# A ring of 12 slots in place of 8 for gathered rows, in memory from the descriptor region

## The chip, the cores and the metric

One Trainium2 chip, one of its cores. The metric is the device time in microseconds (us) of one execution. The engines are called PE (TensorE, matrix products), DVE (VectorE), ACT (ScalarE), POOL (GpSimd) and SP (SyncE, which only issues DMAs).

## The reference

A graph layer with 6250 nodes and 100,000 edges, in float32, on rows of 128 features. The edges are sorted by their target `dst`; `src` is random.

```
hs, hd = x[src], x[dst]
a_k    = exp(relu([hs, hd] @ W_att_k + b_att_k))                 k = 1, 2, 3
avg    = (a_1 / att_1[dst] + a_2 / att_2[dst] + a_3 / att_3[dst]) / 3,   att_k = segment_sum(a_k, dst)
m      = avg * relu(relu(relu(hs @ W1 + b1) @ W2 + b2) @ W3 + b3)
h      = segment_sum(m, dst) / max(degree, 1)
out    = layernorm(x + relu([x, h] @ Wc1 + bc1) @ Wc2 + bc2)
```

The three message layers depend on the source node alone, and so does one half of each attention logit.

## The kernel before

**First stage (to about 55 us).** The messages and the source half of the logits are computed once per node and stored in HBM as a table, one row of 131 floats a node (128 message values and 3 logits, `ROW`). Beside it, POOL gathers plain rows of `x` for nine "early" half units (36 gathers, L558), whose messages are later computed from `x` without the table.

**Edge stage (55 to 776 us).** The 391 groups of 256 edges (`GROUP`, two tiles of 128) are worked off in 126 units (`first_order`, L131). The first unit is one pair of groups, the next 23 are long units of four groups (8 tiles), the other 102 are short ones of two groups (4 tiles; the last one has a single group). Every tile needs one indirect DMA of POOL (L1224) that fetches the 128 table rows which its edges name, 524 bytes each. Nine of the long units (3, 5, ..., 19) gather only their first half, since the other half is an early one: 558 gathers in all.

The gathered rows go to a ring in SBUF, `gath` (L606), of `RING` = 8 slots with 4 tiles each. A long unit takes two places of the ring, any other unit one (`places`, L1066). For every unit POOL waits until PE has finished the units whose slots it needs (L1218, on `s_sum`, which PE raises with the last L1409 matmul of a unit), and then issues the unit's gathers; `taken` (L1069) says which unit that is. Each slot has a semaphore of its own (`s_gath`, L725).

For unit i the other engines work in order:
- SP loads the edges' distances (`near`) and the target half of the logits (`q_eye`).
- PE spreads the target half over the edges (L1357).
- DVE reduces it (L1809), then waits for the gathered rows and adds their three logits (L1815). This is the first read of the ring.
- ACT takes the exponential (L1537) and copies the mask (L1577); DVE makes the weights (L1835, L1840).
- PE multiplies gathered rows and weights into sums (L1405, and L1409 for the attention sums); DVE adds these to `acc` (L1857).

Each engine's order is written out by hand in one loop over the steps i: at step i DVE does L1815 and the weights of unit i + 1, then the sums of unit i - 1, and PE the sums of unit i. A stall of DVE at L1815 holds all of DVE's later work.

Other work is laid between these steps. Steps 0 to 24 count the edges from the first 94 groups ("hot" groups, whose targets are the first 384 nodes) in a table of counts (PE L1426, DVE L1693 and L1706, ACT L1551). Steps 26 to 77 then pass over all 49 blocks of the message table and multiply them by counts times exponentials (PE L1443, ACT L1507 and L1516, DVE L1736); step 78 adds the result to `acc` (DVE L1753). After it the final blocks start: when all edges of 512 nodes are summed, PE (L867, L881, L888, L892, L898), ACT (L917) and DVE (L954, L972, L979, L989, L993) make the output of these nodes in eight steps laid over the next units, and SP loads their `x` ahead and stores the output. The last blocks end at 791.6 us, after the last unit.

A second pass over the edges stands in the code for inputs whose targets don't fit the windows; it does not run here.

All buffers of the edge stage stand one behind the other in one SBUF tile, `work`, of `WORK` = 7536 float32 words a partition; the ring is the first. The program is built with the default region for the descriptors of POOL's DMAs, 16 KB a partition of SBUF.

```
def taken(i, ring):
    return sum(at < place[i] + places[i] - ring for at in place) - 1

def rows_of(i):
    at = place[i] % RING * CHUNK
    return gath[:, at:at + n_tiles(i), :]

for n, u in enumerate(order):
    if taken(n, RING) >= 0:
        pool.wait_ge(s_sum, groups_to(taken(n, RING)))
```

Of the kernel before, what the change touches and what calls it, by code (L numbers as in the profile page):

```python
# [52 lines left out]
HOT_GROUPS = 94  # L53
HOT_WIDTHS = (6, 9, 10)
PAIRS = 4
RING = 8
TWO, THREE = 2, 3
AHEAD = 3
NEAR = 6
# [33 lines left out]
def gnn_program(nc, x, x_t, src, dst, w_first, w_rest, b_rows, table, hot_table, near_table, q_table, early_table, out,  # L93
# [59 lines left out]
    with ctx:  # L153
        def sb(name, shape, dt=f32):
            return ctx.enter_context(nc.sbuf_tensor(name, shape, dt))

        def sem(name):
            return ctx.enter_context(nc.semaphore(name))
# [101 lines left out]
        more = sb("more", [1, 1], i32)  # L260

        WORK = 7536
        work = sb("work", [P, WORK])

        def area(at, *dims):
            n = 1
            for d in dims:
                n *= d
            view = work[:, at:at + n]  # L270
            if len(dims) == 2:
                view = view.rearrange("p (a b) -> p a b", a=dims[0])
            if len(dims) == 3:
                view = view.rearrange("p (a b c) -> p a b c", a=dims[0], b=dims[1])
            if len(dims) == 4:
                view = view.rearrange("p (a b c d) -> p a b c d", a=dims[0], b=dims[1], c=dims[2])
            return view, at + n
# [9 lines left out]
        part_rest, at = area(at, n_blocks, HEADS)  # L287
        assert at <= WORK - COLS

        hot_logit_flat = hot_logit[:, :, :].rearrange("p j d -> p (j d)")
        staged = [logits_or_x[:, 0:COLS], work[:, WORK - COLS:WORK], hot_logit_flat[:, 0:COLS]]
        early_h, early_x, EARLY_BANK = staged[2], staged[1], 3
# [311 lines left out]

        gath, at = area(0, RING * CHUNK, ROW)  # L606

# [16 lines left out]
        hot_block, at = area(at, BLOCKS, 1 + ROW)  # L624
        assert at <= WORK

# [97 lines left out]
        s_least = sem("s_least")  # L724
        s_gath = [sem(f"s_gath{j}") for j in range(RING)]  # L725
        s_fill = sem("s_fill")
# [335 lines left out]
        def edge_pass(first):  # L1062
# [18 lines left out]
            def n_tiles(i):  # L1081
                return len(order[i]) * TILES
# [28 lines left out]
            def early_rows(k):  # L1111

                at = (place[early_units[k]] + 1) % RING * CHUNK
                return gath[:, at:at + CHUNK, 0:P]
# [18 lines left out]
# [5 lines that stand above are left out]
            def tiles_at(i, h):  # L1138

                return 0 if h and early(i) is not None else max(0, min(CHUNK, n_tiles(i) - h * CHUNK))  # L1140

            def rows_landed(eng, i):
                for h in range(places[i]):
                    if not tiles_at(i, h):
                        continue
                    slot = (place[i] + h) % RING
                    eng.wait_ge(s_gath[slot], 16 * sum(tiles_at(n, k) for n in range(i + 1) for k in range(places[n])
                                                       if (place[n] + k) % RING == slot))

# [863 lines left out]
```

## Time and profile before

| | |
|---|---|
| median of 3 runs | 998.15 us |
| lowest, highest run | 995.25, 999.38 us |
| span of the profiled execution | 791.6 us |
| median of the runs less the span | 206.6 us |
| own time of the profiled execution | not given beside its span |
| mean granted clock of TensorE | 0.885 |

Busy tenths of each engine in 40 slices of the span (19.8 us each), with the granted clock of TensorE, the DMA engines' share and what they moved:

```
PE   9952999999986779988889888887978887788885
DVE  5884678778887786777776777776677878787766
ACT  6656687777553426767677667661223233232323
POOL 7777777766577777777777777777777777777760
PEclk9985698988896775999999999999789989889898
DMA  7873333325742233333333333335234334333421
```

The span runs from the program's first to its last instruction on the engines; the rest of a run's time lies around it. A digit is the busy share of a slice in tenths, and 9 is 90% or more; PEclk is the clock that PE was granted, in tenths of full speed. Times in rows count from the span's start. "Idle before, and who ended it" counts only the time in which that engine itself stood still. An indirect DMA's row shows POOL's work on issuing it, not the transfer.

### The profile page before, as it was taken

Reading aid. Unit: us, or ns where it says so; the run is one execution under the profiler, and the core shown is the slowest. Engines: PE = TensorE matmul, PEld = TensorE weight load, DVE = VectorE, ACT = ScalarE, POOL = GpSimd, SP = SyncE. Lnnn points to the kernel's source line nnn. Section 1 sums busy time; section 2 is a strip of 40 time slices with the busy share of each in tenths; the row PEclk is TensorE's granted clock in tenths of the full one; section 3 lists DMA queues with packets and bytes.
Section 4 is the critical chain, followed back from the end, with each engine's and each line's share of the span. In section 5 each row is a group of like instructions: output and inputs, shape, how many; then the busy total and the mean of one; then the engine's idle time right before and its main releaser. Section 6 shows DMA issues by size and latency. Waiting matters only on the chain.

```text
span 791.6 us, 17405 instructions
## 1 busy us (share of the span) xinstructions
PE 663.7 (84%) x5133; PEld 520.8 (66%) x5133; DVE 582.3 (74%) x1943; ACT 420.1 (53%) x1048; POOL 571.1 (72%) x605
## 2 busy tenths in 40 slices
PE   9952999999986779988889888887978887788885
PEld 5741666666654556877778777775766765666664
DVE  5884678778887786777776777776677878787766
ACT  6656687777553426767677667661223233232323
POOL 7777777766577777777777777777777777777760
PEclk9985698988896775999999999999789989889898
DMA  7873333325742233333333333335234334333421
GB/s 241 237 200 78 81 84 80 79 68 62 70 81 58 70 96 75 87 79 78 79 84 80 82 80 78 77 76 135 66 96 111 105 105 134 105 104 104 98 59 34
DMA packets 82741, 75.14 MB, mean 95 GB/s; under 512 B 34872, under 2 KB 66400, under 8 KB 82640
## 3 DMA queue, kind: packets, MB, share of 16 engines
q0 software_dynamic: 19008, 39.82, 22.9%
q1 hardware_dynamic: 63344, 34.00, 15.6%
q8 instruction: 44, 0.72, 0.4%
q14 instruction: 57, 0.47, 0.2%
q10 hardware_dynamic: 288, 0.13, 0.1%
HBM read 64.62 MB, written 9.26 MB: 93 GB/s over the span
## 4 chain that ended last, share of the span: by engine, by line
DVE 30%; PE 27%; issue 14%; ACT 12%; POOL 7%; DMA 5%; DVEq 2%; SPq 1%; ACTq 0%
DVE fin L1736 9%; PE bank L1405 8%; ACT bank L1516 5%; POOL work L1224 5%; DVE acc L1857 3%; PE bank L1426 3%; DVE counts L1706 3%; PE bank L1409 3%; PE bank L881 2%; DVE fin L1693 2%; DVE work L1835 2%; DMA work<-message_table,src_t 2%; DVE fin L972 2%; DVE work L1840 2%; ACT work L1577 2%
## 5 line engine op out<-in xcount | busy, mean ns | idle before, releaser
L1224 POOL DMA_INDIRECT work<-message_table,src_t x558 | 530.2, 950 | 184.3 <-issue 164.8
L1405 PE MATMUL bank<-work 128*128 128x144 f32 (+8 forms) x1188 | 229.4, 322 | 41.7 <-DVE acc L1857 41.3
L1405 PEld LDWEIGHTS bank<-work 128*128 128x128 f32 x1188 | 181.9, 216 | 69.6 <-issue 55.9
L1577 ACT COPY work<-bank 128x192 f32<-128x192 f32 (+7 forms) x126 | 37.3, 296 | 207.1 <-DVE work L1809 206.0
L1443 PE MATMUL bank<-work,fin 128*128 128x129 f32 (+1 forms) x882 | 113.3, 284 | 0.0
L1857 DVE TENSOR_TENSOR acc<-acc,bank 128x192 f32 (+8 forms) x297 | 88.8, 299 | 30.4 <-issue 6.7
L1516 ACT ACTIVATE bank<-hot_logit 128x384 f32<-128x384 f32 (+1 forms) x147 | 72.7, 494 | 69.1 <-DVE fin L1736 61.3
L1443 PEld LDWEIGHTS bank<-work,fin 128*128 128x128 f32 (+1 forms) x882 | 104.2, 195 | 2.4 <-issue 0.6
L1840 DVE TENSOR_TENSOR work<-bank,work 128x576 f32<-128x576 f32 (+7 forms) x126 | 86.2, 684 | 13.5 <-DVE work L1835 0.5
L1736 DVE SCALAR_TENSOR_TENSOR fin<-bank,counts 128x384 f32<-128x384 f32 (+1 forms) x147 | 81.4, 554 | 18.1 <-ACT bank L1516 17.2
L1409 PE MATMUL bank<-work 128*4 128x48 f32 (+8 forms) x1188 | 92.3, 202 | 0.0
L1507 ACT ACTIVATE hot_logit<-logits_or_x,work 128x384 f32<-128x384 f32 (+1 forms) x147 | 88.3, 601 | 0.0
L881 PE MATMUL bank<-rest_w,acc 128*128 128x128 f32 x294 | 50.2, 334 | 29.4 <-DVE fin L972 26.4
L1409 PEld LDWEIGHTS bank<-work 128*4 128x4 f32 x1188 | 48.8, 87 | 35.8 <-issue 7.4
L881 PEld LDWEIGHTS bank<-rest_w,acc 128*128 128x128 f32 x294 | 44.6, 237 | 31.4 <-DVE fin L972 27.5
L1706 DVE TENSOR_TENSOR counts<-counts,bank 128x294 f32 (+2 forms) x94 | 56.2, 598 | 8.3 <-issue 7.3
L1357 PE MATMUL bank<-side 48*128 48x57 bf16 (+8 forms) x594 | 41.3, 185 | 22.6 <-DMA side<-logit_parts 18.0
L1551 ACT ACTIVATE fin<-fin 128x128 bf16<-128x128 f16 x188 | 59.4, 386 | 0.0
L1426 PE MATMUL bank<-fin 128*128 128x294 bf16 (+2 forms) x188 | 48.7, 396 | 11.5 <-ACT fin L1556 8.0
L1835 DVE TENSOR_SCALAR work<-work 128x12 f32<-128x12 f32 (+1 forms) x126 | 24.6, 195 | 42.4 <-ACT work L1537 40.4
L1693 DVE TENSOR_SCALAR fin<-fin 128x294 bf16<-128x294 f16 (+2 forms) x188 | 55.5, 338 | 0.0
L1767 DVE TENSOR_SCALAR side<-side,less_col 48x512 bf16<-48x512 bf16 x149 | 52.3, 364 | 3.3 <-DMA side<-near_nodes 3.2
(150 smaller groups left out, 769.0 us busy)
## 6 DMA issues: line engine op xcount, KB each, us to landing
work<-message_table,src_t POOLq DMA_INDIRECT x558
side<-near_nodes SPq DMA_DIRECT2D x102, 48.0 KB
side<-logit_parts SPq DMA_DIRECT2D x297, 0.8 KB
message_table<-work SPq DMA_DIRECT2D x12, 262.0 KB, 3.6
work<-message_table SPq DMA_DIRECT2D x48, 65.5 KB
work<-in_x_t SPq DMA_DIRECT2D x12, 256.0 KB, 4.2
fin<-in_x SPq DMA_DIRECT2D x11, 256.0 KB, 2.8
logits_or_x<-in_x_t SPq DMA_DIRECT2D x11, 256.0 KB, 3.5
```

Source lines behind the costliest of these rows:

```text
L881: last = pe.matmul(to[:, k * P:(k + 1) * P], acc[:, k, nodes], wc1[:, 1, :], start=True, stop=True)
L1224: pool.indirect_dma_start(out=rows_of(n)[:, t, :], out_offset=None, in_=table[:, :], in_offset=bass.IndirectOffsetOnAxis(ap=src_t[:, h, g: ...
L1405: pe.matmul(sums[:, at:at + HEADS * w], rows_here[:, t, 0:P], wt_of(i)[:, t, :], start=h == 0, stop=h == TILES - 1)
L1409: last = pe.matmul(sums[SUMS_AT:SUMS_AT + HEADS + 1, at + HEADS * w:at + HEADS * w + w], a_col[:, i % THREE, t, :], mask_of(i)[:, t, :], s ...
L1426: pe.matmul(bank[COUNT_BANKS[g % FOUR]][:, 0:n], hot_lo[:, t % HOT_RING, :], hot_comb[:, t % HOT_RING, 0:n], start=h == 0, stop=h == TILES ...
L1443: last = pe.matmul(bank[SIDE_BANKS[h]][:, k * (P + 1):(k + 1) * (P + 1)], hot_wt[0:m, b % THREE, k, h * P:(h + 1) * P], rows_here, start=F ...
L1507: act.activation(hot_logit[0:m, n % TWO, :], hot_ld[0:m, k, :], ACT.Relu, bias=hot_block[0:m, b % BLOCKS, 1 + P + k:2 + P + k]).then_inc(s ...
L1516: act.activation(bank[EXP_BANK][0:m, 0:hot_nodes], hot_logit[0:m, n % TWO, :], ACT.Exp).then_inc(s_he, 1)
L1706: dve.tensor_tensor(here, here, bank[COUNT_BANKS[g % FOUR]][:, 0:w * n_blocks].rearrange("p (b d) -> p b d", d=w), ALU.add).then_inc(s_cad ...
L1736: dve.scalar_tensor_tensor(hot_wt[0:m, b % THREE, k, :], bank[EXP_BANK][0:m, 0:hot_nodes], FLT_MAX, counts[0:m, b, :], ALU.min, ALU.mult). ...
L1840: dve.tensor_tensor(wt_of(i).rearrange("p t (k w) -> p t k w", w=w), from_q(i)[:, :, PARTS:PARTS + w].unsqueeze(2).to_broadcast([P, n, HEA ...
L1857: dve.tensor_tensor(here, here, sums[:, at:at + (HEADS + 1) * w].rearrange("p (k w) -> p k w", w=w), ALU.add).then_inc(s_acc, 1)
```

## The change

The ring gets 12 slots, and with it 12 semaphores in place of 8. The slots are 4 x 131 words each; four more are 2096 words, by which `work` grows to 9632 words (8384 bytes more a partition). The region for the descriptors of POOL's DMAs shrinks from 16384 to 4096 bytes a partition, which frees 12288. Every buffer behind the ring in `work` stands 2096 words further on. Where `RING` is used, the numbers follow: POOL's wait for a slot (`taken`), the slot and the semaphore of a unit, the wait of DVE before it writes early rows to a slot (L1821), and POOL's closing loop (L1228), which waits for the last 12 units' gathers in place of the last 8.

```diff
-RING = 8
+RING = 12
...
-        WORK = 7536
+        WORK = 9632
         work = sb("work", [P, WORK])
...
-    nc = bacc.Bacc("TRN2", target_bir_lowering=False, num_devices=1)
+    nc = bacc.Bacc("TRN2", target_bir_lowering=False, num_devices=1, dynamic_dma_scratch_size=4096)
```

## Rows read from the trace of the kernel before

**Rows 1.** The page: span, and busy us (share) and instructions of each engine
```profile
span 791.6 us, 17405 instructions
PE 663.7 (84%) x5133; PEld 520.8 (66%) x5133; DVE 582.3 (74%) x1943; ACT 420.1 (53%) x1048; POOL 571.1 (72%) x605
```

**Rows 2.** Waits, whole span: who waited for whom, us in total, times, longest
```profile
POOL work L1224 <- PE bank L1409: 19.5, 17, 5.7
DVE work L1815 <- DMA work<-message_table,src_t: 18.7, 12, 4.0
```

**Rows 3.** The gather line: count, ns min/median/max, first and last start
```profile
L1224 POOL DMA_INDIRECT work<-message_table,src_t x558: 938/944/2104, 55.2 to 768.6; - x186
```

**Rows 4.** Waits of POOL in 150 to 263 us
```profile
POOL work L1224 <- PE bank L1409: 16.4, 7, 5.7
```

**Rows 5.** Timeline of POOL: start, us, instruction, idle before and releaser
```profile
164.69 0.94 POOL L1224 DMA_INDIRECT work<-message_table,src_t  x1 [3.69 <-PE bank L1409]
...
270.60 0.97 POOL L1224 DMA_INDIRECT work<-message_table,src_t  x1 [0.30 <-issue]
...
535.50 0.94 POOL L1224 DMA_INDIRECT work<-message_table,src_t  x1 [0.30 <-issue]
```

**Rows 6.** Line L1815 in 290:536, 535:590, 590:745 and 745:792 us, with its waits
```profile
L1815 DVE TENSOR_TENSOR work<-work x53: 170/172/174, 290.3 to 535.7; 128x12 f32<-128x12 f32 x53
...
  DMA work<-message_table,src_t: 7.7, 5
...
  DMA work<-message_table,src_t: 0.6, 1
...
L1815 DVE TENSOR_TENSOR work<-work x6: 167/172/179, 748.5 to 773.9; 128x12 f32<-128x12 f32 x5, 128x6 f32<-128x6 f32 x1
...
  DMA work<-message_table,src_t: 5.3, 4
```

**Rows 7.** Timeline of DVE: first reads of gathered rows
```profile
290.28 0.17 DVE L1815 TENSOR_TENSOR work<-work 128x12 f32<-128x12 f32 x1
...
538.43 0.17 DVE L1815 TENSOR_TENSOR work<-work 128x12 f32<-128x12 f32 x1
...
546.54 0.17 DVE L1815 TENSOR_TENSOR work<-work 128x12 f32<-128x12 f32 x1 [4.03 <-DMA work<-message_table,src_t]
...
578.02 0.17 DVE L1815 TENSOR_TENSOR work<-work 128x12 f32<-128x12 f32 x1 [1.36 <-DMA work<-message_table,src_t]
...
763.61 0.18 DVE L1815 TENSOR_TENSOR work<-work 128x12 f32<-128x12 f32 x1 [2.29 <-DMA work<-message_table,src_t]
```

**Rows 8.** Waits of PE in 554:572, 572:592, 743:764 and 764:792 us
```profile
PE bank L1405 <- DVE acc L1857: 3.4, 1, 3.4
...
PE bank L881 <- DVE fin L972: 4.0, 1, 4.0
...
PE bank L867 <- DVE acc L1857: 2.3, 1, 2.3
PE bank L881 <- DVE fin L972: 0.4, 1, 0.4
...
PE bank L881 <- DVE node_sums L954: 2.8, 1, 2.8
```

**Rows 9.** By stage: us, busy us of each engine, PEclk, DMA share, GB/s
```profile
313.00:536.00 223.00, 197.32 (x1806) 172.44 (x1806) 159.03 (x465) 155.89 (x371) 168.62 (x179) 0.99 0.33 80
536.00:592.00 56.00, 46.65 (x371) 37.54 (x369) 37.47 (x127) 10.62 (x38) 42.28 (x46) 0.82 0.37 98
592.00:743.00 151.00, 124.89 (x994) 101.78 (x992) 119.04 (x432) 46.64 (x152) 114.21 (x121) 0.91 0.42 110
```

**Rows 10.** Timeline of POOL: two of its three longest gathers
```profile
78.89 2.10 POOL L1224 DMA_INDIRECT work<-message_table,src_t  x1 [0.30 <-issue]
...
760.58 1.46 POOL L1224 DMA_INDIRECT work<-message_table,src_t  x1 [0.30 <-issue]
```

**Rows 11.** The early gathers (L558): the longest ones, and issue to landing
```profile
L558 POOL DMA_INDIRECT hot_logit<-in_x,src_t x12: 940/944/1774, 14.9 to 51.3; - x12
...
DMA to landing us min/median/max: 3.2/4.0/4.8
```

## Prediction

> **What bounds the kernel now.** I read the page's busy shares first, then the waits, then the gather line, then the timelines of GpSimd (POOL) and of VectorE (DVE), then TensorE's (PE) waits by stage. In the shares [rows 1] no engine is full: PE is busy for 84% of the span, POOL for 72%. But POOL's share hides a saturated queue. Its 558 gathers take 944 ns each in the median [rows 3] and are 0.30 us apart (the idle in brackets of an undisturbed gather [rows 5] is that), so one leaves each 1.25 us: 558 x 1.25 = 697 us of the 714 us from the first to the last start [rows 3]. The other 17 us are almost all one thing: 19.5 us waited for PE's L1409, the matmul whose end frees a ring slot [rows 2]. In the stretch 150 to 263 us there are seven such waits, 16.4 us [rows 4], the first before the gather at 164.69 [rows 5]; seven usual spaces of 0.30 us are in them, so the ring itself costs 16.4 - 2.1 = **14.3 us** of POOL's time. From 262 us on POOL never stops.
>
> Who suffers? In L1815 DVE adds the gathered logits, so it is the first reader of a unit's rows. It reads unit 25 at 290.28 [rows 7], whose last gather began at 270.60 and ended at 271.57 [rows 5]: 18.7 us ahead. It reads unit 78 at 538.43, whose last gather ended at 536.44: 2.0 us. So between them the consumers (DVE and PE) outrun POOL: 53 units from 290.3 to 535.7 with no wait for rows [rows 6], 245.4 / 52 = 4.72 us each, against 4 x 1.25 = 5.0 us. The lead that POOL had is eaten at about 0.3 us a unit. From then on rows come late: 7.7 us of waits in 535 to 590, 0.6 in 590 to 745, 5.3 in 745 to 792 [rows 6], 13.6 in all of the 18.7 us [rows 2]; the other 5.2 us are the first two units, which the ring can't help. The kernel is consumer-bound until 536 us and short of rows in two places after it.
>
> **The change, part by part.** *Four more slots.* A long unit uses two places, a short one uses one. POOL may now be 12 places ahead of the units that PE has finished, not 8. While the nine early units alternate with the others, four places are one full long unit (8 gathers) and one early one (4): 12 gathers, 12 x 1.25 = 15.0 us; later they are 16 gathers, 20 us. The stalls to cover sum to 14.3 us, so all seven go, just. Two more slots, 7.5 us, would not do. POOL's 406 gathers from 261.9 us then run 14.3 us earlier, as long as PE's times up to 262 us stay as they are; nothing there waits for rows, so I let them stay.
>
> *What the earlier rows are worth.* Not 14.3 us: only where somebody waits for rows and PE, the busiest engine, is idle for it. Wait by wait, the smaller of DVE's wait and PE's idle time behind it:
> - 546.54, 4.03 us [rows 7]. Behind it PE idles 3.4 us before 554.61 [rows 8], and a little more before that. I take 4.0.
> - 563 and 568, 1.5 us together (the rest of the 7.7). PE has no other wait from 554.6 to 572 [rows 8]: it is full, so 0.
> - 572.94 (0.83 us) and 578.02 (1.36 [rows 7]): PE then waits 4.0 us for DVE's L972, which stands behind them [rows 8]. 2.2.
> - 590 to 745: 0.5.
> - Three waits in 745 to 760, 3.0 us: PE waits only 0.4 us after 743.05 [rows 8]. 0.4.
> - 763.61, 2.29 us [rows 7]: PE waits 2.8 us for DVE's L954 right after [rows 8]. 2.3.
>
> The sum is **9.4 us**. The bounds: 13.6 us if PE would have followed DVE everywhere, 14.3 us if POOL's lead counts whole; at the low end the first wait alone, counted by PE's single idle stretch, 3.4 us. Nearest to the rows is the sum itself, as it takes each wait with its own cover.
>
> *TensorE's clock.* From 313 to 536 us the granted clock is 0.99, that is nearly always the upper of the two levels (2.4 GHz); in 536 to 592, with PE waiting for late rows, it is 0.82 [rows 9]. If the waits shrink, the clock may stay up in some of it. I give it nothing in the sum; it is held by the 14.3 us bound, since POOL's rows can come no earlier.
>
> *Tail.* After DVE's last L1815 (773.9 us [rows 6]) there are 17.7 us of closing work, the same before and after. POOL's closing loop waits for 12 units in place of 8, all landed: nothing. The large loads after the hot blocks, which delay the landing behind the 4.03 us wait, hang on DVE's and PE's progress and not on POOL, so they stay where they are, while the rows they delayed will have been fetched 14 us before.
>
> *Smaller descriptor region.* No row prices it. If it never fills, it costs 0. If it fills, POOL stands at the gather until something has landed. A gather from HBM is on the way for 3.2 to 4.8 us from its issue [rows 11], so at 1.25 us a gather at most four are in flight. I take 0: of 558 gathers only three exceed 1.1 us, such as the 2.10 us at 78.89 and 1.46 us at 760.58 [rows 10], at no even distance, so even the large region's end leaves no periodic mark. The upper bound is in the third rival.
>
> *The rest.* Everything behind the ring in the work tile moves by 2096 words: no instruction changes. Between 150 and 262 us the DMA engines get the same gathers a little denser: nothing.
>
> Sum against the profiled span: 791.6 - 9.4 = 782.2 us. Its page has no time of its own beside the span; the median of the runs is 998.15 us, 206.6 us around the span, which I leave alone. **Forecast 998.15 - 9.4 = 988.7 us.**
>
> **Rivals.** *The waits change their name (no change).* DVE no longer waits for rows, but PE is full in 554 to 572 and 743 to 763 and its final blocks wait for DVE's L972. Then only PE's idle 3.4 us before 554.61 is won: 994.7 us. For it: PE at 83% in 592 to 743 [rows 9] with two engines taking turns. Against: the waits before 583 and 766 follow directly on late rows.
>
> *The slots are not used (no change).* If POOL is held by something besides the slot count, its starts stay: 998 us. Against: each of the seven waits ends with L1409 [rows 4], the release that the count sets.
>
> *The small region fills (slower).* Place: L1224 on POOL. The three long gathers and one of 1.77 us among the 36 early ones [rows 11] are perhaps the large region's refills; a quarter of the size makes 16. Price of each: POOL waits until the newest gather has landed, about 1.6 us after its issue ends (DVE's read at 763.61 comes 1.6 us after the end of the gather of 760.58 [rows 7, 10]), less the 0.3 us that it stands anyway, 1.3 us: 21 us; up to a whole landing of 4.8 us, 77 us. Before, POOL's pace was the end's pace in the last stage, so what exceeds the 14.3 us gained is lost: 21 - 14.3 = 6.5 us, 1004.7 us, and up to 1060. It decides from 14.3 / 16 = 0.9 us a refill. Against: in the profile a region of four times the size stops POOL nowhere by more than 1.2 us.
> **How the numbers follow.** About 5.0 us, 0.5%, is what a measurement of this kernel can tell from no change: faster is under 993.2, slower over 1003.1. Forecast case 0.75 (a gain from 5 to 14.3 us), the waits renamed 0.14, slots unused 0.04, region fills 0.07. So faster 0.75, same 0.18, slower 0.07. The range reaches from 998.15 - 14.3 less 1.8 us for the spread of the runs, 982, to 994.7 plus the same 1.8, 996.5; it leaves out the slow rival, most of the unused slots and the tails.
>
> **What would show it.** Right: no wait of POOL for L1409 between 150 and 263 us, the last gather starting near 754 and not 768.6 us; L1815's waits of 13.6 us after 535 us gone, the first two units' 5.2 us still there; DVE's first 78 units within 1 us of before; span near 782 us. The renamed waits show as longer idle times of DVE before L1809 for PE, at an unchanged end. Wrong: gathers with a median over 944 ns or many over 1.1 us (region), or seven waits still there (slots), or times before 290 us that move.

## The result, and the profile after

The change ran at 1025.03 us (median of 4 runs, 1024.09 to 1030.59) beside 998.76 us of the kernel before (4 runs, 995.25 to 1006.12): 1.023 of it, 95% interval 1.0182 to 1.0279. It is slower, by 26 us, where 9.4 us less was forecast.

The profiled execution took 1025.45 us and its span is 1021.6 us: 3.9 us lie around the span, and 3.7 to 4.3 us in each single run below. So nothing like the 206.6 us of the table ahead of the prediction exists. The profile shown of before and the times shown of before belong to two different paces of the same program. The runs below had both: in four sessions (kernels run in turn on one chip) the kernel before took 805 to 809 us, in two others 1008 and 1010 us. One chip number had 1008 us in one session and 809 in a later one, so the pace isn't tied to the number. I call the two "the 805 pace" and "the 1000 pace". The rows ahead of the prediction are of the 805 pace, the 998.76 and 1025.03 us of the 1000 pace.

Page of the change (1000 pace), then its gather line, its L1815 line and its waits for a slot, which answer to [rows 1, 2, 3]:
```profile
span 1021.6 us, 17406 instructions
PE 753.3 (74%) x5133; PEld 585.7 (57%) x5133; DVE 580.7 (57%) x1943; ACT 424.7 (42%) x1048; POOL 569.8 (56%) x605
```
```profile
L1224 POOL DMA_INDIRECT work<-message_table,src_t x558: 939/944/1759, 78.5 to 958.4; - x186
...
  remote: 139.3, 59
  PE bank L1409: 67.8, 26
...
L1815 DVE TENSOR_TENSOR work<-work x126: 167/172/242, 86.0 to 1003.9; 128x12 f32<-128x12 f32 x111, 128x24 f32<-128x24 f32 x14, 128x6 f32<-128x6 f32 x1
...
  DMA work<-message_table,src_t: 1.7, 1
```
A gather takes the same 944 ns. But POOL now stands 207.1 us for others (139.3 + 67.8; "remote" is a release that the records don't resolve), and the last gather starts 45 us ahead of the last read of rows, where it was 5.3 us ahead [rows 3, 6]. Rows are plentiful, and DVE waits for them once, 1.7 us. What a longer ring can give, rows earlier, nobody needs at this pace. Before it is so with 8 slots as well; the kernel before, run again as before_again:
```profile
L1224 POOL DMA_INDIRECT work<-message_table,src_t x558: 938/944/1900, 73.1 to 961.0; - x186
...
  remote: 143.4, 90
...
  PE bank L1409: 80.0, 22
...
L1815 DVE TENSOR_TENSOR work<-work x126: 165/172/186, 84.3 to 986.7; 128x12 f32<-128x12 f32 x111, 128x24 f32<-128x24 f32 x14, 128x6 f32<-128x6 f32 x1
...
  DVE work L1809: 0.9, 2
```
Its last gather starts 25.7 us ahead of the last read, it never waits for rows, and its span is 1004.6 us: that is where the change has to be compared.
```profile
span 1004.6 us, 17405 instructions
```

What does the change lose there? Read VectorE's timeline at unit 3, in which L1767 builds the selection from a load that SP issues: first in the profile shown of before, then before_again, then the change.
```profile
78.44 0.60 DVE L1767 TENSOR_SCALAR side<-side,less_col 48x512 bf16<-48x512 bf16 x2 [3.25 <-DMA side<-near_nodes]
```
```profile
116.44 0.82 DVE L1767 TENSOR_SCALAR side<-side,less_col 48x512 bf16<-48x512 bf16 x2 [19.59 <-issue]
```
```profile
134.06 0.70 DVE L1767 TENSOR_SCALAR side<-side,less_col 48x512 bf16<-48x512 bf16 x2 [36.27 <-issue]
```
The wait grows from 19.6 to 36.3 us with the change, and it's 3.2 us at the 805 pace. The two records of the 1000 pace name no releaser ("issue"). In region_4k, ring8_moved, wait8_2 and ring12_8k below the same wait (22.3, 22.5, 22.5 and 35.0 us) ends with the DMA `side<-near_nodes`, the load that SP issues. What is late is SP. Its timeline, grouped, and POOL's in the same stretch, for the change:
```profile
82.41 27.36 SPq L1252 DMA_DIRECT2D side<-logit_parts  x10
111.88 0.70 SPq L1273 DMA_DIRECT2D hot_logit<-early_rows  x1
115.39 15.75 SPq L1252 DMA_DIRECT2D side<-logit_parts  x8
131.19 0.41 SPq L1240 DMA_DIRECT2D side<-near_nodes  x1
```
```profile
122.22 0.95 POOL L1224 DMA_INDIRECT work<-message_table,src_t  x1 [0.30 <-issue]
129.96 0.94 POOL L1224 DMA_INDIRECT work<-message_table,src_t  x1 [6.79 <-remote]
```
and the same of the profile shown of before:
```profile
62.12 7.99 SPq L1252 DMA_DIRECT2D side<-logit_parts  x10
70.22 0.35 SPq L1273 DMA_DIRECT2D hot_logit<-early_rows  x1
70.94 5.06 SPq L1252 DMA_DIRECT2D side<-logit_parts  x8
76.05 0.41 SPq L1240 DMA_DIRECT2D side<-near_nodes  x1
```
SP needs 27.4 us for ten small loads that took 8.0, and 15.8 for eight that took 5.1; the near load that DVE wants comes at 131.19, eight us after POOL has stopped because its ring is full. At its own pace the kernel before shows what the change adds. In before_again the ten loads take 26.6 us as well; it's the eight behind them that are quick there:
```profile
80.83 26.62 SPq L1252 DMA_DIRECT2D side<-logit_parts  x10
...
108.28 5.49 SPq L1252 DMA_DIRECT2D side<-logit_parts  x8
```
They come after POOL's first pause, 102.86 to 107.47 us. SP's issues are 3.5 to 4.3 us apart from 83.8 to 107.1 us, that is until 4 us into the pause. Then they are 0.7 us apart, also while POOL issues its next gathers. In the change the pause begins at 123.17 us, and SP is back at 0.7 us from 129.4. The register instructions between the loads show the slower pace too. Line L1252 in the profile shown of before, then in the change (ns min/median/max):
```profile
L1252 SPq FUSED_REGOPS  x297: 214/218/251, 61.7 to 747.3; - x149
```
```profile
L1252 SPq FUSED_REGOPS  x297: 2/223/733, 82.0 to 980.3; - x149
```
An instruction that touches a register alone and takes 0.22 us now takes up to 0.73 us. Counted over both kinds of SP's register instructions on this line, 594 in each trace, those over 0.5 us are 39 to 68 in the seven traces of the 1000 pace and none in those of the 805 pace, but for one in hold_after_2. PE has a sign of the pace as well, idle time for which the profile names no one. In the profile shown of before and in after_2 it has none; in before_again, whose expectation asks for 50 us or more of it, it's 108 us in all, half of it here:
```profile
PE bank L1405 <- issue: 55.4, 66, 4.0
```

### The profile page after: what moved, and what is told of

Read it like the earlier page. It is cut to its first block, busy times and chain, and to the rows that moved or that the text cites. A ratio compares the mean times of both kernels' runs of the same rounds, so it can differ in the third digit from the quotient of the medians.

```text
span 1021.6 us, 17406 instructions
## 1 busy us (share of the span) xinstructions
PE 753.3 (74%) x5133; PEld 585.7 (57%) x5133; DVE 580.7 (57%) x1943; ACT 424.7 (42%) x1048; POOL 569.8 (56%) x605
## 2 busy tenths in 40 slices
DMA packets 82741, 75.14 MB, mean 74 GB/s; under 512 B 34872, under 2 KB 66400, under 8 KB 82640
## 4 chain that ended last, share of the span: by engine, by line
PE 47%; issue 21%; DVE 14%; another core or an unknown queue 11%; ACT 5%; DVEq 1%; DMA 0%; SPq 0%; ACTq 0%
PE bank L1405 13%; PE bank L1443 12%; PE bank L1409 4%; PE bank L1426 3%; PE bank L1357 3%; DVE acc L1857 2%; DVE counts L1706 2%; PE bank L881 2%; PE bank L599 2%; DVE fin L972 2%; PE bank L1361 1%; DVE side L1767 1%; PE bank L1379 1%; PE bank L587 1%
## 5 line engine op out<-in xcount | busy, mean ns | idle before, releaser
L1224 POOL DMA_INDIRECT work<-message_table,src_t x558 | 529.9, 950 | 354.3 <-issue 143.8
L1405 PE MATMUL bank<-work 128*128 128x144 f32 (+8 forms) x1188 | 246.5, 340 | 34.2 <-issue 17.4
L1405 PEld LDWEIGHTS bank<-work 128*128 128x128 f32 x1188 | 200.1, 236 | 60.0 <-issue 46.7
L1443 PE MATMUL bank<-work,fin 128*128 128x129 f32 (+1 forms) x882 | 140.6, 320 | 29.7 <-issue 29.7
L1443 PEld LDWEIGHTS bank<-work,fin 128*128 128x128 f32 (+1 forms) x882 | 128.0, 228 | 40.7 <-issue 38.7
L1809 DVE TENSOR_REDUCE work<-bank 128x12 f32<-128x36 f32 (+1 forms) x126 | 24.8, 197 | 158.1 <-remote 70.6
L1409 PE MATMUL bank<-work 128*4 128x48 f32 (+8 forms) x1188 | 98.2, 207 | 14.6 <-issue 14.5
L881 PE MATMUL bank<-rest_w,acc 128*128 128x128 f32 x294 | 54.7, 355 | 48.5 <-DVE fin L972 35.4
L1357 PE MATMUL bank<-side 48*128 48x57 bf16 (+8 forms) x594 | 45.8, 187 | 53.5 <-issue 41.2
L1409 PEld LDWEIGHTS bank<-work 128*4 128x4 f32 x1188 | 50.9, 88 | 51.3 <-issue 24.6
L1426 PE MATMUL bank<-fin 128*128 128x294 bf16 (+2 forms) x188 | 60.0, 471 | 24.6 <-issue 19.6
L1767 DVE TENSOR_SCALAR side<-side,less_col 48x512 bf16<-48x512 bf16 x149 | 50.4, 351 | 36.3 <-issue 36.3
L1357 PEld LDWEIGHTS bank<-side 48*128 48x128 bf16 x594 | 27.5, 96 | 72.6 <-issue 64.6
```

Source lines behind the costliest of these rows:

```text
L881: last = pe.matmul(to[:, k * P:(k + 1) * P], acc[:, k, nodes], wc1[:, 1, :], start=True, stop=True)
L1224: pool.indirect_dma_start(out=rows_of(n)[:, t, :], out_offset=None, in_=table[:, :], in_offset=bass.IndirectOffsetOnAxis(ap=src_t[:, h, g: ...
L1357: last = pe.matmul(from_q(i)[:, t, :], near_of(i)[:, t * P:(t + 1) * P], q_eye[:, slot(i, t // TILES), 0:PARTS + width(i)], start=True, st ...
L1405: pe.matmul(sums[:, at:at + HEADS * w], rows_here[:, t, 0:P], wt_of(i)[:, t, :], start=h == 0, stop=h == TILES - 1)
L1409: last = pe.matmul(sums[SUMS_AT:SUMS_AT + HEADS + 1, at + HEADS * w:at + HEADS * w + w], a_col[:, i % THREE, t, :], mask_of(i)[:, t, :], s ...
L1426: pe.matmul(bank[COUNT_BANKS[g % FOUR]][:, 0:n], hot_lo[:, t % HOT_RING, :], hot_comb[:, t % HOT_RING, 0:n], start=h == 0, stop=h == TILES ...
```

## The experiments

Ratios are to the kernel before on the same chip, each with its 95% interval.

**At the 1000 pace, first session (before 1007.76 us).** *before_again* is the kernel before unchanged.

> The kernel before, unchanged, for a second profile of it. The first profile spans 791.6 us, the runs 998 us, while the changed kernel's profile spans 1021.6 us with runs of 1025 us. If something stands around the span in the kernel before (206 us), this profile spans about 792 us again. If the profiled execution was an unusually short one, it spans about 994 us, with the waits that the changed kernel's profile also shows: PE idle for no reason that the profile names, 50 us or more before L1357 and L1405.

Measured: 0.998 [0.9944, 1.0018], span 1004.6 us, so nothing stands around the span. *region_4k* has only `dynamic_dma_scratch_size=4096`.

> Ring of 8 and all buffers as before; only the descriptor region is 4 KB and not 16. Theory A (the small region costs the time): slower by 2.3% or more, about 1021 us. Theory B (ring, or where the buffers lie, costs it): within 0.5% of 998 us.

Measured: 1.0112 [1.0071, 1.0154], between the two theories. *ring12_8k* has a region of 8 KB beside the 12 slots.

> Ring of 12 as in the change, but the descriptor region is 8 KB and not 4. Theory A: if the cost goes with the number of times that the region is filled, half of it is gone, about 1011 us, and less than 1005 us if 8 KB is large enough. Theory B: as slow as the change, about 1025 us.

Measured: 1.0201 [1.016, 1.0241]. *ring8_moved* undoes the ring alone (the memory stays moved):
```
-RING = 12
+RING = 8
```

> The change with RING set back to 8: the region of 4 KB and a work tile of 9632 words, the last COLS words of which hold early_x, stay as in the change; the buffers behind the ring stand where they did before relative to the tile. Theory A: about 1021 us, as region_4k. Theory B, ring: 998 us; B, place of the tile's end: 1025 us.

Measured: 1.0147 [1.0099, 1.0195]. So at this pace the small region, or the addresses that it shifts, costs 1.1 to 1.5 per cent with 8 slots, and with 12 slots the kernel is 2.0 slower even with a region twice as large. Neither part gives anything. That the slots cost something of their own these ratios don't settle, as the intervals of ring8_moved and ring12_8k overlap; the traces further down do for the head of the edge stage.

**Next session (before 807.55 us).** Made to test the head of the edge stage, it met the 805 pace. *wait8* turns back the one wait:
```
-                        if taken(n, RING) >= 0:
-                            pool.wait_ge(s_sum, groups_to(taken(n, RING)))
+                        if taken(n, 8) >= 0:
+                            pool.wait_ge(s_sum, groups_to(taken(n, 8)))
```

> The change with one thing turned back: POOL waits before a gather as if the ring had 8 slots (12 are there and are used in turn). Theory A, the run-ahead: with 12 slots POOL issues 36 gathers without a pause at the head of the edge stage in place of 24, and SP, whose first loads go out slowly until POOL pauses, is that much later; then the one_hot of L1767 waits some 22 us as with 8 slots, not 36, POOL pauses after gather 24, and the time is 1.010 to 1.016 of the kernel before. Theory B, the place or number of the slots: 12 slots in use cost it, whoever waits; then the time stays at 1.020 to 1.026 though the pause comes after 24.

Measured: 0.9932 [0.9882, 0.9983], with 18.7 us of waits for rows at L1815, as before. *region_pad* keeps every address:
```
+        sb("unused", [P, 3072])
...
-    nc = bacc.Bacc("TRN2", target_bir_lowering=False, num_devices=1)
+    nc = bacc.Bacc("TRN2", target_bir_lowering=False, num_devices=1, dynamic_dma_scratch_size=4096)
```

> The kernel before with the descriptor region of 4 KB in place of 16 and an unused array of 12 KB a partition ahead of all others, so that every array keeps the address it has in the kernel before. Theory region: the smaller region itself costs the 1.1 per cent of the run with ring 8 and 4 KB; the time is 1.008 to 1.015 of the kernel before. Theory address: it was the 12 KB by which all arrays moved down; the time is 0.997 to 1.003.

Measured: 0.9999 [0.9958, 1.0041]. *hold_before* and *hold_after* stop POOL once, in the kernel before and in the change:
```
+                        if first and n == 2:
+                            pool.wait_ge(s_ein, 16)
```

> The kernel before, but POOL waits once, ahead of the gathers of unit 2, until the load of the edge inputs that SP issues first has landed. Theory A (gathers issued without a pause slow SP's issuing): SP issues its first loads at its usual pace, L1767's wait falls from 19.6 us to under 8 us, the stage's early units come 10 to 15 us sooner, and the time is 0.985 to 0.992 of the kernel before. Rival (SP is slow at this place for a reason of its own, or the time is set elsewhere): L1767's wait stays near 20 us or the time stays within 0.997 to 1.003.

> The change with the same single wait of POOL ahead of the gathers of unit 2. Theory A: L1767's wait falls from 36 us to under 10 us, and with it what 12 slots cost beyond the smaller region and more: the time is 0.990 to 1.003 of the kernel before, level with hold_before but for the region's per cent. Rival (12 slots cost time throughout, not at the head of the stage): the time falls by no more than 0.5 per cent from 1.023.

Measured: 1.002 [0.9967, 1.0074] and 0.9878 [0.9826, 0.993]. The first missed its number because SP isn't slow at this pace: L1767 waits 3.5 us. The second is a surprise only to one who has the 1.023 in mind: with 12 slots the kernel is faster here.

**The change itself at the 805 pace (before 807.16 us).**

> The change itself once more, beside the next three kernels and the kernel before. So far it ran only where the kernel before takes some 1000 us, and there it took 1.023; where the kernel before takes some 805 us it was not tried. Theory A (what the ring of 12 gives or costs depends on whether rows are scarce or plentiful, and that on which of the two paces the chip runs): beside 805 us the ratio is 0.985 to 0.995, L1815's waits for rows after 536 us are gone and L1767 waits under 5 us; beside 1000 us the ratio is 1.018 to 1.028 and L1767 waits some 36 us. Theory B (the change costs its 2 per cent everywhere): 1.015 or more beside either.

Measured: 791.99 us, 0.9814 [0.9755, 0.9873], a little more gain than the 0.985 to 0.995 expected; L1767 waits 3.2 us. Its gather line and L1815:
```profile
L1224 POOL DMA_INDIRECT work<-message_table,src_t x558: 941/947/2027, 55.6 to 759.4; - x186
...
  PE bank L1409: 5.2, 9
...
L1815 DVE TENSOR_TENSOR work<-work x126: 167/172/212, 66.7 to 766.3; 128x12 f32<-128x12 f32 x111, 128x24 f32<-128x24 f32 x14, 128x6 f32<-128x6 f32 x1
...
  DMA work<-message_table,src_t: 1.9, 1
```
POOL's waits for a slot are down from 19.5 to 5.2 us, DVE's for rows from 18.7 to 1.9 us [rows 2], and the span is 783.2 us.

> The change with 8 slots left in use, the memory moved and the region at 4 KB. Theory A: beside 805 us it is level with the kernel before, 0.995 to 1.003, so that what the change gives comes from the 12 slots; beside 1000 us it repeats 1.010 to 1.020. Theory B: 1.010 or more beside either.

Measured: 0.9993 [0.9923, 1.0063], with the waits back:
```profile
POOL work L1224 <- PE bank L1409: 25.5, 14, 5.4
DVE work L1815 <- DMA work<-message_table,src_t: 19.3, 13, 3.8
```
So at this pace the gain comes from the 12 slots, and the region costs nothing that the runs can tell. Over all sessions of this pace the seven ratios of kernels in which POOL waits as with 8 slots are 0.993 to 1.005. Two of them, wait8 and region_pad_2, have intervals that leave out 1, so some 0.5 per cent of a ratio may be scatter. The five with 12 slots are 0.977 to 0.988. *region_pad_2* and *hold_after_2* repeat kernels:

> The region of 4 KB with an unused array of 12 KB ahead, so that all addresses stay. Beside 805 us it was 0.9999; a repeat gives 0.995 to 1.004. Beside 1000 us: theory region, 1.007 to 1.015, as with the region alone; theory address, 0.996 to 1.003.

> The change with POOL's one wait ahead of unit 2's gathers. Beside 1000 us: if gathers issued without a pause slow SP's issuing at the head of the edge stage, L1767's wait falls from 36 us to under 10 us and the ratio from 1.023 to 0.990 to 1.008; if not, it stays above 1.018. Beside 805 us SP is not slow there and the hold costs at most its 4 us of POOL: the ratio repeats 0.983 to 0.993 and stands within 0.4 per cent of the change without the hold.

Measured: 0.9949 [0.991, 0.9988] and 0.9846 [0.979, 0.9903]. The hold is level with the change (0.9814) within the intervals.

**A session at the 805 pace again (before 805.25 us)** repeated two kernels:

> The change with POOL's one wait ahead of unit 2's gathers, meant for a chip on which the kernel before takes some 1000 us. There: if gathers issued without a pause slow SP's issuing at the head of the edge stage, L1767's wait falls from 36 us to under 10 us and the ratio from 1.023 to 0.990 to 1.008; if SP is slow there by itself, the wait stays over 25 us and the ratio above 1.018; if the wait falls and the ratio does not, the head of the stage is not what the change loses there. Beside 805 us the ratio repeats 0.985, with L1767 at some 3.6 us.

> The region of 4 KB with an unused array of 12 KB ahead, so that all addresses stay. Beside 1000 us: theory region, 1.007 to 1.015, as the region alone gave there (1.011); theory address, 0.996 to 1.003. Beside 805 us it was 0.9999 and 0.9949 and would be 0.995 to 1.002.

Measured: hold_after_3 0.9865 [0.9811, 0.9918], region_pad_3 1.0047 [0.9992, 1.0101], a little over the 1.002 expected.

**The 1000 pace again (before 1010.27 us).**

> As hold_after_3, once more for a chip on which the kernel before takes some 1000 us. There: L1767's wait under 10 us and the ratio 0.990 to 1.008 if POOL's gathers without a pause hold SP back at the head of the edge stage; wait over 25 us and ratio above 1.018 if SP is slow there by itself. Beside 805 us: 0.983 to 0.990 again.

Measured: 1.0289 [1.014, 1.0439]. The wait fell as the first theory says, to 8.1 us, but the ratio stayed where the rival has it. The timelines say why. SP (the first two lines), then DVE (L1769, L1811 and L1817 here are L1767, L1809 and L1815 of the change), then POOL's two pauses:
```profile
81.53 14.44 SPq L1254 DMA_DIRECT2D side<-logit_parts  x10
96.81 5.13 SPq L1254 DMA_DIRECT2D side<-logit_parts  x8
...
105.42 0.61 DVE L1769 TENSOR_SCALAR side<-side,less_col 48x512 bf16<-48x512 bf16 x2 [8.09 <-DMA side<-near_nodes]
...
150.78 0.23 DVE L1811 TENSOR_REDUCE work<-bank 128x24 f32<-128x72 f32 x1 [31.72 <-remote]
151.12 0.17 DVE L1817 TENSOR_TENSOR work<-work 128x12 f32<-128x12 f32 x1
...
99.53 0.94 POOL L1226 DMA_INDIRECT work<-message_table,src_t  x1 [6.58 <-DMA hot_logit<-early_rows]
```
With POOL halted from 92.9 to 99.5 us, SP's ten loads take 14.4 us in place of 27.4 and its eight 5.1 in place of 15.8, and L1767's wait is 8.1 us in place of 36.3. Then POOL runs on for 36 gathers without a pause, to 145.6 us, and now PE crawls. Its matmuls there, for which the profile names no releaser, start 2.1 to 2.8 us apart:
```profile
130.39 0.19 PE L1411 MATMUL bank<-work 128*4 128x20 f32 x1 [2.53 <-issue]
132.50 0.19 PE L1411 MATMUL bank<-work 128*4 128x20 f32 x1 [1.92 <-issue]
135.29 0.19 PE L1411 MATMUL bank<-work 128*4 128x20 f32 x1 [2.60 <-issue]
137.40 0.19 PE L1411 MATMUL bank<-work 128*4 128x20 f32 x1 [1.91 <-issue]
```
From 148.6 us, 3 us after POOL's last gather of that stretch, they stand 0.7 us apart. Unit 3's rows are read at 151.1 us; in the change they are read at 145.6. The hold moved the loss from SP to PE, and didn't remove it.

> The change with POOL waiting as with 8 slots. Beside 1000 us: if POOL's longer stretch without a pause is what 12 slots cost, L1767 waits some 22 us and the ratio is 1.010 to 1.016, as with 8 slots and a 4 KB region; if it is the slots, 1.020 to 1.026. Beside 805 us: the gain of the 12 slots is gone, 0.993 to 1.002, against 0.981 of the change, if the run-ahead is what gives it.

Measured: 1.0125 [0.9991, 1.0259], L1767 22.5 us: what was expected of the run-ahead, though its interval holds 1.023 too and the ratio alone decides nothing. The traces do. All of the 1000 pace, in us:

| kernel | gathers before POOL's first full ring | POOL's first gather | end of that stretch | unit 3 read | from first gather to unit 3 | unit 3 to the end of the span |
|---|---|---|---|---|---|---|
| before_again | 24 | 73.1 | 102.9 | 128.2 | 55.0 | 876.4 |
| region_4k | 24 | 79.5 | 109.2 | 132.5 | 53.0 | 877.1 |
| ring8_moved | 24 | 77.6 | 107.3 | 130.8 | 53.2 | 884.9 |
| wait8_2 | 24 | 70.6 | 100.3 | 125.4 | 54.9 | 887.2 |
| ring12_8k | 36 | 68.8 | 113.6 | 138.0 | 69.2 | 874.0 |
| the change | 36 | 78.5 | 123.2 | 145.6 | 67.1 | 876.0 |

Unit 3 comes 22 to 25 us after POOL's first pause in all six. Four slots more are twelve gathers more before it, 12 x 1.25 = 15 us [rows 5], and the head is 12 to 16 us longer. After the head the traces with 12 slots aren't longer than those with 8. Against before_again the change's span is 17.0 us longer: 5.4 before POOL's first gather, 12.1 in the head, -0.4 after it. These are single executions, and the time up to POOL's first gather varies by 11 us among them; but wait8_2 and the change differ in nothing but POOL's wait, and its head is 12 us shorter.

**Last session (805 pace, before 809.11 us).** *late12* keeps 12 slots for later units only:
```
-                        if taken(n, RING) >= 0:
-                            pool.wait_ge(s_sum, groups_to(taken(n, RING)))
+                        ahead = 8 if n < 12 else RING
+                        if taken(n, ahead) >= 0:
+                            pool.wait_ge(s_sum, groups_to(taken(n, ahead)))
```

> The change with POOL waiting as with 8 slots for the first 12 units and as with 12 from there. Beside 1000 us: if what 12 slots cost there is the head of the edge stage alone, POOL pauses first after 24 gathers, L1815's unit 3 comes some 53 to 55 us after POOL's first gather (67 to 73 with 12 slots from the start), and the ratio is that of 8 slots with a 4 KB region, 1.010 to 1.017, not 1.023; if 12 slots cost time all along, 1.020 or more with the early unit 3 all the same. Beside 805 us POOL does not stall in the first 12 units anyway: the gain of the change stays, 0.978 to 0.988.

Measured: 0.9773 [0.9681, 0.9864]. The gain doesn't need the slots in the head, and within the intervals late12 is as good as the change here; whether it saves the head at the 1000 pace wasn't measured.

> The region of 4 KB with all addresses as before. Beside 1000 us: theory region, 1.007 to 1.017; theory address, 0.996 to 1.004. Beside 805 us: 0.995 to 1.005, as its three runs there gave.

Measured: 1.0009 [0.9949, 1.0069].

## Why the prediction was wrong

**The step that failed** is "206.6 us around the span, which I leave alone". The rows came from an execution 206 us shorter than the runs. That difference isn't time around the kernel: the profiled execution of before_again took 1008.54 us and spans 1004.6, so 3.9 us lie around it. It's another pace of the kernel itself, in which the premise "short of rows in two places after it" doesn't hold. The sum that follows was made for an execution that the timed runs didn't have. The gap was in the table, larger than every effect discussed, and should have been a case of its own: if the span of the runs is some 994 us, POOL's 697 us of gathers can't be near the bound, and no ring gives anything.

**Ring stalls, 14.3 us, and the lead.** At the 805 pace right in kind. POOL's waits for L1409 in after_2: 5.2 us in all, the last start 759.4 us (forecast near 754), later by 5.4 us: 0.4 from the later begin, 1.7 from gathers 3 ns longer (558 x 3 ns), 3.0 from two waits that are left in 150 to 263 us (2.8 and 0.8 us, less their 0.30), where none was forecast. DVE's waits for rows after 535 us are gone, as forecast. POOL has nearly no pause between 55.6 and 760 us now: there it is the bound.

**The worth of the rows, 9.4 us.** Mis-sized at the 805 pace, low: 807.16 x 0.0186 = 15.0 us, interval 10 to 20. Two terms were small. The shown execution, 791.6 + 3.9 = 795.5 us, lies below all the 84 timed ones of the kernel before at this pace (798 to 831); the other profiles there in which POOL waits as with 8 slots have spans of 792.5 to 825.4 us. And *the clock, 0*, is probably too low: in 536 to 592 us the granted clock was 0.82 [rows 9] and is 1.00 in after_2:
```profile
313.00:536.00 223.00, 196.21 (x1771) 170.21 (x1769) 160.28 (x466) 157.44 (x374) 168.67 (x179) 0.98 0.35 80
536.00:592.00 56.00, 48.28 (x447) 38.93 (x447) 44.41 (x147) 15.98 (x52) 42.39 (x45) 1.00 0.41 101
```
In the same 56 us PE makes 447 matmuls in place of 371, though the program is further on by then. One pair of traces proves little: over all traces of this pace the clock in that stretch is 0.79 to 0.94 where POOL waits as with 8 slots (eight traces, mean 0.87) and 0.91 to 1.00 with 12 (five, mean 0.95). PE's waits of 3.4 and 4.0 us there [rows 8] fell to 1.6 and 1.8. 15.0 us also lies a little over the 14.3 us that the prediction took as the clock's bound, though the interval holds both.

**Region, 0.** Right at the 805 pace: four runs of region_pad (0.995 to 1.005) and ring8_moved_2. In after_2 7 of POOL's 594 gathers exceed 1.1 us, against 5 before, the longest 2.03 us: no mark of a region that fills. At the 1000 pace three kernels with 4 KB in which POOL waits as with 8 slots stood at 1.011, 1.015 and 1.013 (the last with an interval that holds 1). Whether that is its size or the shifted addresses is open, as region_pad never met this pace.

**The slow rival** was right in sign only. Its place, L1224 waiting for the region, isn't where the change was seen to lose; the part of the loss that was located is before L1767, 36.3 us, a wait that the prediction doesn't name, since it took 3.2 us in the profile shown. **"Nothing"** for the denser gathers between 150 and 262 us stands at the 805 pace; that a longer stretch of gathers can make other engines slower was not thought of.

**What stays open.** Why the program has two paces, and why SP and PE crawl at the slower one while POOL runs without pause at the head. DMA bandwidth isn't short: the same 75.14 MB move at 74 GB/s in place of 95, and packets keep the DMA engines busy for 32% of the change's span, 39% of the one shown of before. Nor is it TensorE's clock alone: one execution of the kernel before in the sessions of the 805 pace had a mean of 0.769 and took 813.55 us. And it doesn't go with POOL's running throughout: from 160 us to POOL's last gather, PE's idle time for which the profile names no one is 0.07 to 0.15 us per us while POOL runs and 0.19 to 0.25 while it is paused, in the seven traces. The Trainium skill (NOTIFIC — the notification-queue block, 7.1 Overflow: three behaviours, one of which stalls the engine) says that the block which writes the profiler's records holds its producers back when its inner buffers are full ("always backpressures rather than losing a record inside the block"); that could slow engines without a wait, but no run here shows it. The head explains some 12 to 16 of the 26 us. The rest is of the size of the 11 us (1.1 per cent) that region_4k lost, and was located in no trace.

## What to carry to other kernels

Check first that the profile is of the time that you want to explain: span plus a few us must be the run's time, and a gap of 200 us is a case of its own and no constant. A deeper ring gives only where its consumer waits for rows (L1815 waits 18.7 us for them: yes; it waits for none and the producer stands 223 us: no), and it lengthens the first stretch in which the producer runs without a pause. If the early units need another queue's small loads, let the depth grow after the head, as late12 does at no loss at the pace where it ran.

## What the runs showed of the hardware that was not expected

The same program ran at 798 to 831 us in four sessions and at 995 to 1020 us in the others, with a mean granted clock of 0.84 to 0.89 (once 0.77) and of 0.75 to 0.78. At the slower pace SP's register instructions, 0.22 us at the other, took up to 0.73 us in the change and up to 1.4 us in before_again and region_4k, and PE's matmuls without a wait came 2.1 to 2.8 us apart (125 to 147 us of hold_after_4), each until POOL had paused for 2 to 6 us (before_again, the change, hold_after_4), while GpSimd's gathers kept their 944 ns and 0.30 us spacing. One change was 1.9 per cent faster at one pace and 2.3 slower at the other.
